# Attention as one stream of 16 head pairs, with the output projection and the weight quantisation inside the pairs

## The reference, cut to what matters

```python
q = (resid_pre @ Wq.T).reshape(b, s, H, DH)          # H = 16 heads, DH = 128
k = (resid_pre @ Wk.T).reshape(b, s, H, DH)
v = (resid_pre @ Wv.T).reshape(b, s, H, DH)
scores = jnp.einsum('bqhd,bkhd->bhqk', q, k) / math.sqrt(DH)
scores = jnp.clip(scores, -1024.0, 1024.0)
scores = scores + _alibi_mask(H, s, s)[None]
attn = jax.nn.softmax(scores.astype(jnp.float32), axis=-1)
z = jnp.einsum('bhqk,bkhd->bqhd', attn, v)
out = jnp.einsum('bqhd,ohd->bqo', z, Wo.reshape(d, H, DH))
...
def ternary_quant(w_fp32, g=64):
    w = w_fp32.astype(jnp.bfloat16)
    w_g = w.reshape(-1, g)
    scale = jnp.clip(jnp.mean(jnp.abs(w_g), axis=-1, keepdims=True), 1e-08, None)
    q = jnp.clip(jnp.round(w_g / scale), -1, 1)
    w_hat = (q * scale).reshape(w.shape)
    return w + jax.lax.stop_gradient(w_hat - w)
...
x = x + _L0_attn_ref(_layernorm(x), Wq, Wk, Wv, Wo)
x = x + _L0_ffn_ref(_layernorm(x), w_gate_up, w_proj)   # both weights through ternary_quant
```

## Time and profile before

| | us |
|---|---|
| runs of the kernel, median (lowest, highest) | 1941.84 (1941.32, 1942.98) |
| the profiled execution, its own time | 1944.27 |
| its span, first to last instruction | 1942.5 |
| PE busy | 1770.2 (91%) |
| DVE busy | 1243.0 (64%) |
| ACT busy | 1137.7 (59%) |
| POOL busy | 617.4 (32%) |
| mean granted TensorE clock | 0.971 of 2.4 GHz |

### The profile page before, as it was taken

One profiled execution on the slowest core, in us unless ns is written; L12 is line 12 of the kernel. 1 busy time (PEld: TensorE's weight loads), 2 busy tenths in 40 slices (PEclk: granted clock), 3 DMA queues, 4 the chain that ended last, 5 costly groups with the idle time before them and its releaser, 6 DMA issues. The chain is left out here.

```text
span 1942.5 us, 29259 instructions
## 1 busy us (share of the span) xinstructions
PE 1770.2 (91%) x8976; PEld 1328.6 (68%) x8976; DVE 1243.0 (64%) x1979; ACT 1137.7 (59%) x2083; POOL 617.4 (32%) x501
## 2 busy tenths in 40 slices
PE   5999999998999999999989898879898799896997
PEld 4777777776787777777768687656456565565886
DVE  3655555564235655555645565888887788876997
ACT  2655555665126655655642454699994899862332
POOL 2232232322113222322220011039792088772000
PEclk9999999999999999999989899889999899998999
DMA  3000000000000000000001100022220122220000
GB/s 120 17 16 16 16 0 16 16 16 1 17 1 17 16 16 16 16 0 16 0 1 65 45 0 1 3 76 98 83 90 1 46 92 92 80 105 1 11 16 17
DMA packets 19959, 61.91 MB, mean 32 GB/s; under 512 B 2304, under 2 KB 6400, under 8 KB 19136
## 3 DMA queue, kind: packets, MB, share of 16 engines
q1 hardware_dynamic: 19904, 61.21, 8.9%
HBM read 58.84 MB, written 2.36 MB: 32 GB/s over the span
## 5 line engine op out<-in xcount | busy, mean ns | idle before, releaser
L1550 POOL TENSOR_SCALAR prob<-prob,rinv 128x128 f32<-128x128 f32 (+7 forms) x256 | 202.5, 791 | 690.0 <-DVE rinv L1160 688.2
L1618 POOL TENSOR_TENSOR m_h<-m_h,m_C 128x1024 f32<-128x1024 f32 x128 | 305.8, 2393 | 200.9 <-DVE m_h L1410 200.9
L1149 DVE TENSOR_SCALAR prob<-ps 128x128 f32<-128x128 f32 (+7 forms) x256 | 192.3, 751 | 240.7 <-PE ps L421 240.7
L456 PE MATMUL ps<-pt,v_sb 128*128 128x512 f32 (+3 forms) x768 | 320.3, 509 | 20.8 <-ACT pt L836 20.8
L1410 DVE TENSOR_TENSOR_SCAN m_h<-m_y,ps 128x1024 f32<-128x1024 f32 x128 | 291.6, 2284 | 53.6 <-PE ps L711 45.7
L836 ACT ACTIVATE pt<-ps 128x512 f32<-128x512 f32 (+3 forms) x384 | 181.9, 489 | 183.9 <-PE ps L445 182.7
L718 PE MATMUL ps<-m_h,ident 128*128 128x512 f32 x512 | 249.9, 612 | 11.0 <-POOL m_h L1618 11.0
L828 ACT ACTIVATE prob<-prob,nmax 128x128 f32<-128x128 f32 (+7 forms) x256 | 198.1, 774 | 83.4 <-DVE nmax L1154 82.3
L1154 DVE CUSTOM_DVE_ANT_0 prob<-prob,bias 128x128 f32<-128x128 f32 (+7 forms) x256 | 194.3, 759 | 44.3 <-issue 22.5
L1025 ACT ACTIVATE m_u<-m_uT,m_bT 128x256 f32<-128x256 f32 x512 | 210.8, 497 | 8.6 <-PE ps L711 8.4
L445 PE MATMUL ps<-ident,prob 128*128 128x128 f32 x1152 | 193.5, 276 | 15.0 <-POOL prob L1550 15.0
(11 more groups left out here) (197 smaller groups left out, 3087.0 us busy)
## 6 DMA issues: line engine op xcount, KB each, us to landing
m_C<-bc_dram SPq DMA_DIRECT2D x64, 512.0 KB, 3.6
wqk_raw<-wqk_in SPq DMA_DIRECT2D x16, 512.0 KB, 3.4
wv_raw<-wv_in SPq DMA_DIRECT2D x16, 256.0 KB, 3.5
x<-x_in SPq DMA_DIRECT2D x2, 1024.0 KB, 7.1
wo_sb<-wo_in SPq DMA_DIRECT2D x1, 2048.0 KB, 11.0
q_raw<-wgu_in SPq DMA_DIRECT2D x1, 2048.0 KB, 7.7
raw<-wgu_in SPq DMA_DIRECT2D x1, 2048.0 KB, 7.6
out<-x SPq DMA_DIRECT2D x8, 256.0 KB, 2.1
```

The lines of the kernel that those rows point to most:

```text
L456: mm = nc.tensor.matmul(ps[:, 6 + g, r0 * P:BANK], v_sb[:, j, u * DH:(u + 1) * DH], pt[:, idx % 3, r0 * P:BANK], start=(j == 0), stop=(j = ...
L1149: nc.vector.tensor_scalar(tile, flat[:, o:o + n], CLIP, -CLIP, ALU.min, ALU.max).then_inc(s_read, 1)
L1550: nc.gpsimd.tensor_scalar(prob[:, at:at + n], prob[:, at:at + n], rinv[:, k:k + 1], 1.0, ALU.mult, ALU.mult).then_inc(norm_done, 1)
L1618: nc.gpsimd.tensor_tensor(state, state, m_C[:, v, :], ALU.mult).then_inc(hc_done, 1)
```

## The change

The two batches become one stream of 16 pairs (`LAST_PAIR` = 15); `a_xh` and `a_xl` exist once per batch, and batch 1 is normalised at the start, into its own tile `a_xn1` and banks 4 to 7. Q/K of batch 1's first pair is made inside batch 0's last pair.

`z` now goes to `z_hi` (ACT) and `z_lo` (DVE, `z_rest`), for two heads only. `pe_out(pe, p, m, ...)` multiplies the two heads of one pair by `wo_hi`/`wo_lo` in three fp32r passes, 24 matmuls for each half m of the tokens, into `s_bank(m)`; it is worked in the next pair, after scores 4 and 5, and `residual` adds it to `x`. Its weights come per pair by DMA; ACT makes `wo_hi`, POOL `wo_lo`.

Quantisation goes in 16 chunks of 512 (batch 0's pairs) or 256 columns (batch 1's), one per pair, into `q_out`. The barrier `PH_O1` and the code between it and `PH_A` go, except the transposes, whose 12 copies ACT and DVE now share. At the start `pool_norm` of batch 0 stands ahead of the splits.

```diff
-            if b:
-                pe_out(pe, b - 1, (0, 1))
-            pe_norm(pe, b, a_xn)
...
+        def pe_out(pe, p, m, count):
+
+            pe.wait_ge(s_read, count)
+            if m == 0:
+                pe.wait_ge(wo_lo_s, p + 1)
+                pe.wait_ge(z_read, p * 4 + (4 + 2))
+            for t in range(4):
+                tok = (4 * m + t) * P
+                cols = ps[:, s_bank(m) + t // 2, (t % 2) * D:(t % 2 + 1) * D]
+                seq = [(a, w, u) for u in range(2) for a, w in passes()]
+                for i, (a, w, u) in enumerate(seq):
+                    mm = nc.tensor.matmul(cols, (z_hi, z_lo)[a][:, u, tok:tok + P], (wo_hi, wo_lo)[w][:, u, :],
+                                          start=(i == 0), stop=(i == len(seq) - 1))
+            mm.then_inc(o_full, 1)
...
+                pe_v(pe, p, b)
+                for k in (4, 5):
+                    pe_scores(pe, p, k, v_read, p * 2 + (k - 3))
+                if begin:
+                    pe.wait_ge(n_lo, 8)
+                else:
+                    for m in range(2):
+                        pe_out(pe, p - 1, m, B0 + (m + 1))
+                pe_values(pe, p, 0, 0, {0: [score_after_out(6)], 1: [score_after_out(7)]})
...
+            body(LAST_PAIR, 1, None)
+            for m in range(2):
+                pe_out(pe, LAST_PAIR, m, base(LAST_PAIR) + (11 + m))
...
+                exps(p, 4)
+                exps(p, 5)
+                pts(p, 0, 0, 0)
+                exps(p, 6)
+                pts(p, 0, 0, 1)
+                exps(p, 7)
+                pts(p, 0, 0, 2)
+                pts(p, 0, 0, 3)
+                z(p, 0, 0)
+                q_magnitudes(p, b)
+                if not last:
+                    split_v(p + 1)
+                    qk(p + 1, 0, B0 + QK_USE[0])
+                    qk(p + 1, 1, B0 + QK_USE[1])
+                split_out(p)
...
+                if not begin:
+                    z_rest(p - 1, 1, 1)
+                q_start(p, b)
+                scores(p, 4, B0)
+                scores(p, 5, B0 + 1)
+                recip(p, 4)
+                if not begin:
+                    for m in range(2):
+                        residual(p - 1, before, m)
+                recip(p, 5)
+                scores(p, 6, B0 + 2)
+                scores(p, 7, B0 + 3)
+                recip(p, 6)
+                recip(p, 7)
+                z_rest(p, 0, 0)
+                q_scales()
                 if not last:
-                    head_bias(p + 1, 0)
+                    head_bias(p + 1, nb, 0)
                     qk(p + 1, 0)
+                    q_signs()
                     qk(p + 1, 1)
...
                 four(p, 8, B0 + use_of(8, last))
+                z_rest(p, 0, 1)
                 four(p, 12, B0 + use_of(12, last))
+                z_rest(p, 1, 0)
                 if not last:
-                    head_bias(p + 1, 1)
+                    head_bias(p + 1, nb, 1)
                     qk(p + 1, 2)
+                    q_values()
                     qk(p + 1, 3)
                     four(p + 1, 0, B0 + NEXT_SCORES)
...
+                def values():
+                    after()
+                    did(nc.vector.tensor_tensor(q_pos[:, 0:n], q_pos[:, 0:n], q_neg[:, 0:n], ALU.subtract))
+                    after()
+                    did(nc.vector.tensor_tensor(groups(q_pos), groups(q_pos), per_group(q_scale), ALU.mult))
+                    after()
+                    did(nc.vector.tensor_tensor(q_pos[:, 0:n], q_pos[:, 0:n], q_bf[:, 0:n], ALU.subtract))
+                    after()
+                    at = (p - PAIRS * b) * n + NGU * b
+                    did(nc.vector.tensor_tensor(q_out[:, bass.ds(at, n)], q_bf[:, 0:n], q_pos[:, 0:n], ALU.add))
```

More of the change, by code:

```diff
@@ new lines, in body @@
+                split_out(p)
+                for j in range(8):
+                    pts(p, 0, 1, j)
+                    if 1 <= j <= 4:
+                        exps(p, 8 + j - 1)
+                z(p, 0, 1)
+                pts(p, 1, 0, 0)
+                exps(p, 12)
+                pts(p, 1, 0, 1)
+                exps(p, 13)
+                pts(p, 1, 0, 2)
+                pts(p, 1, 0, 3)
+                z(p, 1, 0)
+                exps(p, 14)
+                exps(p, 15)
+                if not last:
+                    qk(p + 1, 2, B0 + QK_USE[2])
+                    qk(p + 1, 3, B0 + QK_USE[3])
@@ L875, in act_attention @@
+                for j in range(8):
+                    pts(p, 1, 1, j)
+                    if 1 <= j <= 4 and not last:
+                        exps(p + 1, j - 1)
+                z(p, 1, 1)
+            split_qk(0)
+            split_v(0)
+            act_norm(act, 0, a_xh[0])
             for m in range(4):
-                qk(first, m, 20 * first + m)
+                qk(0, m, m)
             for k in range(4):
-                exps(first, k)
-            with act.Fori(0, PAIRS - 1) as it:
-                body(it + first, False)
@@ L881, in act_attention @@
-            body(first + PAIRS - 1, True)
+                exps(0, k)
+            act_norm(act, 1, a_xh[1], 4)
+            with act.Fori(0, PAIRS) as it:
+                body(it, 0)
+            with act.Fori(PAIRS, LAST_PAIR) as it:
+                body(it, 1)
+            body(LAST_PAIR, 1, last=True)
         def act_ffn_weights(act, hi, cols):
@@ L1170, in four, with z_rest, residual @@
                 recip(p, k0 + 3)
[L1172 to L1174 removed]
+            def z_rest(p, u, g):
+                dve.wait_ge(z_split, p * 4 + (2 * u + g + 1))
+                cols = slice(g * BANK, (g + 1) * BANK)
+                nc.vector.tensor_tensor(z_lo[:, u, cols], ps[:, 6 + g, :], z_hi[:, u, cols].bitcast(F32),
+                                        ALU.subtract).then_inc(z_read, 1)
+            def residual(p, b, m):
+                dve.wait_ge(o_full, p * 2 + (m + 1))
+                dve.wait_ge(o_added, p * 2)
+                rows = x[:, b * TILES + 4 * m:b * TILES + 4 * m + 4, :].rearrange("p t d -> p (t d)")
+                nc.vector.tensor_tensor(rows, ps[:, s_bank(m):s_bank(m) + 2, :].rearrange("p a n -> p (a n)"), rows,
+                                        ALU.add).then_inc(o_added, 1)
@@ new lines, in dve_attention @@
+            qk(0, 0)
+            qk(0, 1)
+            dve_norm_xn(dve, 1, 1, a_xn1)
+            qk(0, 2)
+            qk(0, 3)
+            four(0, 0, 4)
+            dve_norm_lo(dve, 1, a_xl[1], a_xh[1], 4)
+            body(0, 0, 0, begin=True)
+            with dve.Fori(1, PAIRS - 1) as it:
+                body(it, 0, 0)
+            body(PAIRS - 1, 0, 1)
+            body(PAIRS, 1, 1, before=0)
+            with dve.Fori(PAIRS + 1, LAST_PAIR) as it:
+                body(it, 1, 1)
+            body(LAST_PAIR, 1, None)
@@ L1210, in dve_mamba_residual @@
+            z_rest(LAST_PAIR, 1, 1)
+            for m in range(2):
+                residual(LAST_PAIR, 1, m)
         def dve_mamba_residual(dve, b):
```

438 lines of the change are left out of this document (217 added, 221 removed).

## The result

The changed kernel takes **1984.51 us** (median of 4 runs, 1979.73 to 1985.67) against 1941.58 us before in the same series (4 runs, 1940.87 to 1942.98): a ratio of 1.0214, 95% interval 1.0201 to 1.0226, so 43 us slower. The forecast was 1970 us, range 1927 to 2000. The profiled execution took 1979.73 us (span 1977.9).

What follows compares the result with a forecast made beforehand. PE, busy 91% of the span, was read first; pairs were followed with new waits. Terms summed to 1124.1 us at the first gate matmul against 1095.76, +28.3 on the 1941.84 median: 1970 us, range 1927 to 2000.

Steps and rivals of the forecast that it cites:

- start: Up to pair 0's first value matmul: 6.7 us of DVE waiting go, 1.9 of transposes come; 37.4 us.
- Pair 0: First pair, without output matmuls to cover ACT's new order: 64.2 us.
- Fourteen pairs: The steady pairs: seven at 67.7 us in batch 0 and seven at 67.1 in batch 1.
- Last pair with tail: Last pair 61.4 us, then 17.5 to the first FFN gate matmul.
- the rival: PE's clock falls to half behind the new gap in all 15 pairs: +25 us, 1995; chance 0.08.
- (a): First half of head 0: Q/K starts 8.88 us later, 5.85 output matmuls and 3.03 new wait.
- covered residual adds: DVE's two residual adds in (a), hidden by PE's output matmuls; about 2.4 us if those were gone.
- (b): Second half of head 0: wo_hi on ACT costs 0.5 us; q_abs, sums and signs cost nothing.
- (c): Start of head 1: z_lo of head 0 on DVE ahead of score 12; 0.2 us reaches PE.
- (d): Second Q/K: z_lo and value steps on DVE delay k; +0.95 us in batch 0, +0.35 in batch 1.
- Ends: Outside the steady pairs: start 37.4 us, pair 0 64.2, last pair 61.4, then 17.5 to the first gate matmul.
- PE stays the bound: Rival: the wait in (a) is hidden, pairs near 63.0 us, total 1898; chance 0.25.

Runs made afterwards that it cites:

- The control: The changed kernel run again unaltered, beside the runs with one wait filled; 1982.75 us, ratio 1.0205.
- the fills: Changed kernel with redundant transposes in PE's two waits of head 0's first half: both 1971.85 us, first alone 1971.72, second alone 1972.89.
- The second experiment: Changed kernel with the four value steps of the quantisation on DVE moved behind the next pair's scores 0 to 3; 1964.92 us, ratio 1.0103.
- the ACT-order run: Changed kernel with ACT making the pt copies and z_hi ahead of exponentials 6 and 7; 1961.88 us, ratio 1.0089.
- nothing left out: Changed kernel with pt copies and z_hi ahead of exponentials 6 and 7, quantisation sums and signs at pair start, values behind next scores 0 to 3; 1915.98 us.

## Why the prediction was right, and where it was not

**Direction and size.** The forecast put the first gate matmul at +28.3 us; the profile has +35.7. By its own terms (forecast, then measured): start 37.4, 37.96. Pair 0 64.2, 65.55, with a stretch of half clock. Fourteen pairs 943.6, 952.28. Last pair with tail 78.9, 75.63. The 8.7 us in the fourteen pairs are the six disturbed ones at 1.45 each; all undisturbed ones lie within 0.1 us of 67.7 and 67.1, save two that are 0.15 shorter. So the clock was wrong in both: the forecast gave it nothing, the rival gave it all 15 pairs. I gave the rival 0.08 because the pieces of the gap are shorter than in the earlier trace rows; 0.8 and 1.5 us were enough in about half the pairs. Its price of 1.7 us each was close to the 1.45 measured. The control and the fills on one chip put the clock at 10 to 11 us of the 40 that were lost there. The rest of the way from 1970 to 1984.5 is the choice of executions: these terms make 7.3 us, the profiled execution of the kernel before lay 2.4 us above its median and that of the changed kernel 4.8 us below its own. The control's own profile has two more disturbed pairs and a start 2.0 us later.

**(a)** Forecast 8.88 us, measured 8.38 (output matmuls 5.76, waits 2.62). That the waits come of the exponentials ahead of the last `pt` copies is shown: with ACT's order changed and nothing else, Q/K starts 2.6 us earlier. That the late score 6 is needed too is argued from the chain of rows; no run moves the output matmuls alone. The covered residual adds were right: with two thirds of the cover removed, 1.9 of the 3.8 us are lost again, where the forecast had about 2.4 with all of it gone.

**(b), (c)** Forecast 0.7, measured 0.60: the stretch from the end of one Q/K to the start of the next is 20.30 us against 19.70. Not tested apart.

**(d)** Under-sized. The last stage is 13.69 us in batch 0 and 13.04 in batch 1 against 12.03: +1.66 and +1.0, forecast 0.95 and 0.35. DVE in the pair at 240.59:

```profile
292.74 0.69 DVE L1229 TENSOR_TENSOR z_lo<-ps,z_hi 128x512 fp32r<-128x512 f32 x1
293.34 1.32 DVE L1187 TENSOR_SCALAR bias<-ramp,slopes 128x1024 f32<-128x1024 f32 x1
294.59 1.20 DVE L1194 SCALAR_TENSOR_TENSOR qk_lo<-ps,qk_hi 128x1024 fp32r<-128x1024 f32 x1
295.72 0.41 DVE L1282 TENSOR_TENSOR q_pos<-q_pos,q_neg 128x512 bf16<-128x512 bf16 x1
296.16 0.69 DVE L1284 TENSOR_TENSOR q_pos<-q_pos,q_scale 128x512 bf16<-128x512 bf16 x1
296.89 0.42 DVE L1286 TENSOR_TENSOR q_pos<-q_pos,q_bf 128x512 bf16<-128x512 bf16 x1
297.46 0.43 DVE L1289 TENSOR_TENSOR q_out<-q_bf,q_pos 128x512 bf16 x1
297.80 1.22 DVE L1197 TENSOR_TENSOR qk_lo<-ps,qk_hi 128x1024 fp32r<-128x1024 f32 x1
```

The value steps take 2.0 us with their gaps, not 1.65 (the forecast's own parts, 3 x 0.33 + 0.6, add up to 1.59), and the bias 1.32, where it took 0.75 before. The second experiment shows what this stage owes to the value steps: with them moved it takes 12.14 us, 0.1 more than before, though `z_lo` and the long bias still stand there. The errors in (a) and (d) cancelled, 0.5 too much and 0.65 to 0.7 too little in a pair; that the periods came within 0.1 us of the forecast is luck.

**Ends.** In the last pair the forecast took off 3.8 us of POOL's waits between the halves of head 0; all of PE's waits for POOL there fell from 7.5 to 4.1 us, about that. The output projection began 60.68 us into the pair, where the terms gave 63.2. Most of that 2.5 us is the clock again, the other way: the forecast took off 1 us for one half-speed stretch less. In windows of 1 us the kernel before spends about 13.6 us of its last pair at a granted clock of 0.50, the changed kernel 6.8. At half speed that is 3.4 us of work time less (an estimate from these windows). Tail: 14.95 against 15.7.

**The rival "PE stays the bound"** was wrong as a forecast and right as a possibility. It gave 1898 us with pairs of 63.0. Put in free places, the same work runs at 63.6 and 1910 to 1916 us, so the change's loss is one of order, not of work. Its statement that the exponentials alone decide was too simple: freed of them, 1.6 to 2.1 of 2.6 us returned through DVE's queue, since "nothing" for the sums and signs held only under PE's wait. The prediction named that work and what covered it, but not its price with the cover gone.

## What to carry to other kernels

When work goes into a pipelined loop, ask first what late result it pushes back, and what stands behind that result on the other engines' lists. Here the late scores did no harm once nothing that PE needed stood behind their exponentials. A term costed at nothing is nothing only for the present bound; mending a wait of 2.6 us here brought out another of 1.6 to 2.1 us on the next engine, so both have to be moved together. And a wait on PE can cost twice, once as idle time and once as half clock afterwards.

## What the runs showed of the hardware

- **Two short waits lower the clock, one does not.** In two profiles of the changed kernel the granted clock fell to 0.50 in 7 and in 9 of the 15 pairs (1 to 15) with waits of 0.8 and 1.5 us and 1.0 us of work between them; with either filled by transposes it fell behind them in none. Waits of 0.54 and 2.17 us, in pair 0, were enough too, those of 0.53 and 1.08 us were not. In the ACT-order run, with waits of 1.8 us at score 8 and 0.6 (batch 1) or 1.1 us (batch 0) at score 10, it fell in 3 of the first 15 pairs; with nothing left out and the matmuls ahead, where no wait in pairs 1 to 14 is over 0.73 us, in none. The kernels with one wait filled by redundant transposes were 10 and 11 us faster than the control on the same chip.
- **These DVE `tensor_scalar`s, with their operands in SBUF, wait for the POOL operation in progress.** The bias above starts at 293.34 and ends at 294.66 (1.32 us; 0.75 before). In the changed kernel all 15 biases of the second Q/K took 1.32 to 1.37 us, each beside a POOL operation that was already running, and all 15 of the first Q/K 0.75, with POOL idle; in the run with nothing left out POOL runs beside both, and both take 1.32 to 1.38. In the ACT-order run an operation on 4 columns took 1.22 us, 729.79 to 731.01, and in the run with nothing left out one took 1.51 us, 608.93 to 610.44. POOL in order of time, first row of the changed kernel:

```profile
293.00 1.12 POOL L1681 TENSOR_SCALAR prob<-prob,rinv 128x1024 f32<-128x1024 f32 x1 [0.37 <-DVE rinv L1217]
```

then of the ACT-order run and of the run with nothing left out:

```profile
729.70 1.29 POOL L1664 TENSOR_TENSOR wv_lo<-wv_raw,wv_hi 128x512 fp32r<-128x512 f32 x1
```

```profile
608.02 2.40 POOL L1656 TENSOR_TENSOR wqk_lo<-wqk_raw,wqk_hi 128x1024 fp32r<-128x1024 f32 x1 [2.64 <-ACT wqk_hi L831]
```

These end at 294.12, 730.99 and 610.42; the DVE operation ends 0.02 us after POOL where it is small, 0.54 us after it where it has 1024 columns. The Trainium skill, "SBUF — State Buffer", section "Who interferes with whom", says that DVE in a two-port mode and GpSimd take a shared port pair in turn, each for a whole instruction, and that `tensor_scalar` can enter such a mode; these rows agree. With that, the bias would have been priced about 0.6 us dearer. Set against the 0.35 us that the value steps lacked, that is the larger part of what (d) lacked, by this sum and not by a run of its own.
